# An audio tower layer on one core: identity matmuls at the start, first scores before second queries, VectorE normalising the first and last batch, GpSimd rounding the integer weights

## The reference

```python
proj = other @ W1 + readout @ W2 + b          # W1, W2: 256 x 256
h = gelu(proj)                                # 255 x 256
q, k, v = split(layernorm(h) @ qkv_w.T)       # 16 heads of 64
attn = softmax(q @ k.T * 64 ** -0.5 + bias)   # bias: emb_weight[T5 bucket(k - q)]
h = h + (attn @ v) @ o_w.T
g, u = x @ wg.T, x @ wu.T                     # x = layernorm(h); int weights / 127
h = h + (silu(g) * u) @ wd.T                  # hidden 768
```

## Time and profile before

| | us |
|---|---|
| median of 3 runs | 1811.13 (1810.99 to 1811.48) |
| the profiled execution's own time | 1811.56 |
| span of its profile | 1809.3 |
| TensorE (PE) busy | 1766.2 (98%), 17434 matmul instructions |
| VectorE (DVE) busy | 1515.6 (84%) |
| ScalarE (ACT) busy | 1396.9 (77%) |
| GpSimd (POOL) busy | 1167.8 (65%) |
| DMA from issue to landing, medians | bias rows' write 4.3, readout rows' write 2.3, bias read 4.2, pieces of w_v 3.8 |
| ScalarE's high half of a whole-number piece, 512 or 256 columns | 0.62, 0.41 |
| chain that ended last, share of the span | PE 95%, DVE 3%, ACT 1%, issue 1% |

### The profile page before, as it was taken

The page is one execution under the profiler, slowest core; times in us unless marked ns, Lnnn a source line. Parts: engine busy times, 40 slices in busy tenths (PEclk is TensorE's granted clock), DMA queues, the critical chain, the costliest instruction groups (busy, mean ns, idle before and its releaser), DMA issues.

```text
span 1809.3 us, 47269 instructions
## 1 busy us (share of the span) xinstructions
PE 1766.2 (98%) x17434; PEld 1648.3 (91%) x17434; DVE 1515.6 (84%) x4828; ACT 1396.9 (77%) x3795; POOL 1167.8 (65%) x1488
## 2 busy tenths in 40 slices
PE   7899999999999999999999999999999999999996
PEld 5789999999999999999999999999999999999995
DVE  4888888888888888888888888888889888889884
ACT  4877778777778777787777787777787777877873
POOL 2566567666667666667666667666667666667664
PEclk8999999999999999999999999999999999999998
DMA  5200000000000000000000000000000000000000
GB/s 181 71 11 16 16 10 9 14 16 16 16 7 11 16 16 16 16 4 14 16 16 16 16 4 13 16 16 16 16 5 13 16 16 16 16 5 13 8 7 13
DMA packets 26761, 34.13 MB, mean 19 GB/s; under 512 B 3457, under 2 KB 20370, under 8 KB 26530
## 3 DMA queue, kind: packets, MB, share of 16 engines
q1 hardware_dynamic: 26368, 30.95, 5.7%
q10 hardware_dynamic: 98, 0.07, 0.0%
q0 software_dynamic: 64, 0.07, 0.0%
HBM read 22.65 MB, written 8.42 MB: 17 GB/s over the span
## 4 chain that ended last, share of the span: by engine, by line
PE 95%; DVE 3%; ACT 1%; issue 1%; POOL 0%; DMA 0%; POOLq 0%; ACTq 0%; DVEq 0%
PE ps L480 57%; PE ps L561 14%; PE ps L537 13%; PE ps L550 7%; PE ps L489 3%; PE ps L505 2%; DVE prob L958 1%; DVE pT L966 1%; ACT prob L786 0%; POOL normed L410 0%; ACT pT L793 0%; DMA emb_sb<-emb 0%; DVE wu L897 0%; ACT xt L753 0%; DVE v L944 0%
## 5 line engine op out<-in xcount | busy, mean ns | idle before, releaser
L419 POOL TENSOR_TENSOR prob<-prob,inv 128x510 f32<-128x510 f32 x512 | 524.8, 1039 | 371.6 <-DVE inv L971 371.6
L793 ACT ACTIVATE pT<-ps 128x512 fp32r<-128x512 f32 x512 | 278.5, 597 | 322.4 <-PE ps L550 322.3
L786 ACT ACTIVATE prob<-prob,neg_top 128x255 f32<-128x255 f32 x1024 | 506.8, 502 | 5.0 <-DVE neg_top L958 4.7
L958 DVE CUSTOM_DVE_ANT_0 prob<-ps,bias 128x255 f32<-128x255 f32 x1024 | 380.1, 420 | 98.8 <-PE ps L537 91.5
L480 PE MATMUL ps<-xnT,wqk 128*128 128x256 f32 x3072 | 417.0, 285 | 2.9 <-DVE qk L936 1.5
L480 PEld LDWEIGHTS ps<-xnT,wqk 128*128 128x128 f32 x3072 | 381.8, 189 | 15.2 <-issue 1.8
L966 DVE TENSOR_TENSOR pT<-ps,pT 128x512 fp32r<-128x512 f32 x512 | 334.5, 685 | 1.5 <-ACT pT L793 1.5
L561 PE MATMUL ps<-pT,v 128*128 128x256 f32 x2048 | 294.9, 287 | 20.3 <-DVE pT L966 11.2
L561 PEld LDWEIGHTS ps<-pT,v 128*128 128x128 f32 x2048 | 263.7, 190 | 37.6 <-issue 31.8
L537 PE MATMUL ps<-qk 64*128 64x256 f32 x3072 | 252.5, 297 | 0.8 <-DVE neg_top L958 0.8
L537 PEld LDWEIGHTS ps<-qk 64*128 64x128 f32 x3072 | 198.9, 186 | 35.7 <-issue 1.8
(11 more groups left out here) (93 smaller groups left out, 2592.0 us busy)
## 6 DMA issues: line engine op xcount, KB each, us to landing
xt<-x_cols SPq DMA_DIRECT2D x32, 256.0 KB, 2.6
out<-xt SPq DMA_DIRECT2D x32, 128.0 KB, 1.7
r_rows<-readout_rows SPq DMA_DIRECT2D x30, 128.0 KB, 2.9
out<-xt SPq DMA_DIRECT2D x32, 112.0 KB, 1.8
bias<-bias_rows SPq DMA_DIRECT2D x8, 384.0 KB, 4.2
staged<-w_qk SPq DMA_DIRECT2D x8, 256.0 KB, 4.3
staged<-w_v SPq DMA_DIRECT2D x4, 256.0 KB, 3.8
staged<-w_o SPq DMA_DIRECT2D x4, 256.0 KB, 4.9
```

The lines of the kernel that those rows point to most:

```text
L419: pool.tensor_tensor(pr, pr, by, ALU.mult).then_inc(prob_done, 1)
L786: ex = act.activation(pr, pr, ACT.Exp, bias=neg_top[:, g % 2, hh, t:t + 1], scale=-1.0, accum_out=total[:, g % 2, hh, t:t + 1])
L793: act.activation(transposed(0, half), transposed_in(half), ACT.Copy).then_inc(pT_hi, 1)
L958: ins = dve.tensor_tensor_reduce(prob[:, g % 2, hh, t, 0:S], ps[:, bank_s[hh], t * T:t * T + S], falling(2 * g + hh, WINDOW - 1 - b0), 1.0 ...
```

## The change

- TensorE: `keep_busy(n)` issues n matmuls of the 128 x 128 identity by itself, into the bank of queries and keys, whose result nobody reads. `keep_busy(8)` runs first of all, as soon as the identity is made; `keep_busy(5)` stands after the last batch's transposes in `finish`. The bias rows come after `tokens(0)`, and the transposes of batch 0 before the readout rows of all batches. In step 0 `queries_keys(0, 1)` comes after `values(0, 0)` and `scores(0, 0)`. In steps 256 to 259 `down(30)` comes after `project`.
- VectorE: normalises batch 0 and batch 31 (the first and the last layer norm alone), in place of GpSimd. In step 0 it does the low half of `values(0, 0)` and the bias of pair 0 before the low half of pair 1. `output(30)` moves from step 258 to 259, after the statistics of batch 31. The low halves of pieces 16 to 26 come one step later.
- GpSimd: writes the high halves of pieces 16 to 26 (`integer_high`, a tensor_copy from int32 to the rounded format) at the end of steps 3 to 9, where ScalarE wrote them. Its two DMAs go to ScalarE's queue, the one of the bias rows behind gelu(0), that of the readout rows behind the loading of the table for the exponential, ahead of step 0.
- ScalarE: pieces 2, 4 and 5 earlier in the start; the table for the exponential is loaded after the high half of queries and keys of pair 0, not before; `sum_lo` one step later.
- SyncE's queue: piece 5 is asked for before the bias rows.

```diff
@@ -198,6 +198,7 @@
 POOL_PIECES = (13, 14, 15)
+FIRST_INT = min(integer_pieces)
@@ -217,6 +218,7 @@
 piece_hi = sem("piece_hi")
+int_hi = sem("int_hi")
@@ -348,9 +350,10 @@
         load_piece(QK_FIRST)
+        load_piece(QK_FIRST + 1)
...
         load_bias(0)
-        for n in range(NST, len(pieces)):
+        for n in range(V_FIRST, len(pieces)):
@@ -386,8 +389,6 @@
         pool.memset(prob[:], 0.0).then_inc(consts, 1)
-        pool.wait_ge(rel_out, 1)
-        pool.dma_start(rel_dram[:, 0:REL], rel_sb[:]).then_inc(rel_stored, 16)
@@ -431,10 +432,11 @@
+        def integer_high(n):
+            pool.wait_ge(piece_in[n % NST], 16 * (n // NST + 1))
+            pool.tensor_copy(pieces[n][1], stage(n)).then_inc(int_hi, 1)
...
         layer_rstd(0, 0)
-        normalise(0, 0)
-        pool.wait_ge(r_out, 1)
-        pool.dma_start(r_dram, r_sb[:]).then_inc(r_stored, 16)
@@ -464,9 +466,11 @@
                     piece_low(n)
+            for n in PIECES_AT.get(G, ()):
+                if n >= FIRST_INT:
+                    integer_high(n)
...
         run(step)
-        normalise(1, B - 1)
@@ -497,6 +501,10 @@
             pe.matmul(dst, ones_row[:], b_row[:], start=False, stop=True).then_inc(row_mm, 1)
...
+        def keep_busy(n):
+            for _ in range(n):
+                pe.matmul(ps[:, bank_qk, 0:P], ident[:], ident[:], start=True, stop=True)
@@ -654,6 +662,9 @@
             def transpose_banks_free():
+                if G == 1:
+                    pe.wait_ge(pre_done, 2)
+                    pe.wait_ge(r_out, 1)
@@ -680,10 +691,11 @@
-            if pair(G + 1):
+            if pair(G + 1) and G > 0:
...
                 queries_keys(*pair(G + 1))
-            early()
+            if i < B:
+                early()
@@ -693,9 +705,13 @@
                 project(bb, gg)
+            if i == B:
+                early()
...
                 scores(i, g)
+            if G == 0:
+                queries_keys(0, 1)
@@ -703,29 +719,29 @@
             norm_transposed(1, B - 1)
+            keep_busy(5)
...
+        pe.wait_ge(consts, 5)
+        keep_busy(8)
+        pe.wait_ge(r_in, 48)
+        readout_row(0)
+        pe.wait_ge(w1_in, 16)
+        tokens(0)
...
                   ).then_inc(rel_mm, 1)
-        pe.wait_ge(r_in, 48)
-        pe.wait_ge(consts, 5)
-        readout_row(0)
-        pe.wait_ge(w1_in, 16)
-        tokens(0)
...
         tokens(1)
+        norm_transposed(0, 0)
...
                   ).then_inc(r_mm, 1)
-        norm_transposed(0, 0)
         queries_keys(0, 0)
-        pe.wait_ge(pre_done, 2)
-        pe.wait_ge(r_out, 1)
@@ -833,9 +849,11 @@
                 tanh(i - 1, 5)
+            if G == 0:
+                values_hi(0, 0)
...
                 queries_keys_hi(*pair(G + 1))
-            if g == 0 and i < B:
+            if g == 0 and 0 < i < B:
@@ -845,8 +863,8 @@
                 norm_hi(0, i + 1)
-            for n in PIECES_AT.get(G - 1, ()):
-                if n in integer_pieces:
+            for n in PIECES_AT.get(G - 2, ()):
+                if n >= FIRST_INT:
@@ -859,7 +877,8 @@
             for n in PIECES_AT.get(G, ()):
-                piece_high(n)
+                if n < FIRST_INT:
+                    piece_high(n)
@@ -869,17 +888,21 @@
         piece_high(1)
+        piece_high(2)
         gelu(0)
+        act.wait_ge(rel_out, 1)
+        act.dma_start(rel_dram[:, 0:REL], rel_sb[:]).then_inc(rel_stored, 16)
+        piece_high(3)
         row_copied(1)
-        piece_high(2)
-        piece_high(3)
+        piece_high(4)
+        piece_high(5)
...
         gelu(1)
+        queries_keys_hi(0, 0)
...
         act.activation(table[:, 0:1], table[:, 1:2], ACT.Exp).then_inc(table_set, 1)
-        queries_keys_hi(0, 0)
-        piece_high(4)
-        piece_high(5)
+        act.wait_ge(r_out, 1)
+        act.dma_start(r_dram, r_sb[:]).then_inc(r_stored, 16)
@@ -892,7 +915,10 @@
             _, hi, lo, _, _, _, scale = pieces[n]
-            dve.wait_ge(piece_hi, n + 1)
+            if n < FIRST_INT:
+                dve.wait_ge(piece_hi, n + 1)
+            else:
+                dve.wait_ge(int_hi, n - FIRST_INT + 1)
@@ -923,6 +949,14 @@
             ins.then_inc(ln_var[n], 1)
...
+        def normalise(n, batch):
+            dve.wait_ge(ln_rstd[n], count(1, batch))
+            src = token_tile(batch)
+            for t in range(TT):
+                ins = dve.tensor_scalar(normed[:, t, :], src[:, t, :], mean_var[:, n, t, 0:1],
+                                        rstd[:, n, t:t + 1], ALU.subtract, ALU.mult)
+            ins.then_inc(ln_done[n], 1)
@@ -1020,7 +1054,7 @@
                 layer_sums(0, i + 1, gelu_done)
-            if g == 2 and i >= 2:
+            if g == 2 and 2 <= i < B:
@@ -1043,22 +1077,31 @@
                 gating(i - 1, 5)
+            if G == 0:
+                values_lo(0, 0)
+                add_bias(0, 0, 0)
...
                 queries_keys_lo(*pair(G + 1))
-            if g == 0 and i < B:
+            if g == 0 and 0 < i < B:
...
                 layer_var(1, i - 1)
+            if g == 3 and i == B:
+                output(B - 2)
+                normalise(1, B - 1)
...
                 heads_added(*pair(G - 2))
-            if pair(G):
+            if pair(G) and G > 0:
...
             for n in PIECES_AT.get(G, ()):
-                if n not in POOL_PIECES:
+                if n < FIRST_INT and n not in POOL_PIECES:
+                    piece_low(n)
+            for n in PIECES_AT.get(G - 1, ()):
+                if n >= FIRST_INT:
@@ -1070,23 +1113,24 @@
+        piece_low(0)
+        piece_low(1)
+        pre_gelu(0)
...
                           ).then_inc(rel_out, 1)
-        pre_gelu(0)
-        piece_low(0)
...
         layer_var(0, 0)
-        piece_low(1)
...
         piece_low(3)
+        normalise(0, 0)
         pre_gelu(1)
+        norm_lo(0, 0)
+        piece_low(4)
+        piece_low(5)
+        queries_keys_lo(0, 0)
...
         dve.tensor_copy(r_sb[:], ps[0:B, bank_t[0], 0:D]).then_inc(r_out, 1)
-        norm_lo(0, 0)
-        queries_keys_lo(0, 0)
-        piece_low(4)
-        piece_low(5)
```

## The result

The changed kernel takes 1801.09 us (median of 6, 1800.01 to 1802.67) against 1811.31 (1810.84 to 1813.84): ratio 0.9939, 95% interval 0.9928 to 0.9949, 10.2 us less (the quotient of the two medians alone would be 0.9944). Forecast were 11.7 less and 1799.4, in a range of 1796.0 to 1804.5. The profiled execution took 1802.05, its span 1799.9, so span against span it is 9.4 us. Of all executions in this document one, of e1, took 7500.4 us for a reason that no trace shows; it is left out of e1's ratio.

A forecast was written before the change was run, and what follows sets the result against it. TensorE, busy 90% or more except at the edges, bounds the kernel; chains at both ends can move the time. -8.7 - 0.5 - 2.5 = -11.7 from 1811.13 gives 1799.4 us, range 1796.0 to 1804.5.

The forecast's parts named there:

- The start: Up to the second bias of pair 0: earlier high clock, VectorE's shorter normalise and transposes before readout rows, -8.7 us.
- DMAs hidden: In the start, pieces 10 and 11 land 3.8 us after issue, before ScalarE needs them, with 0.4 us to spare.
- Steps 2 to 12: After the start: ScalarE's relief gains little, VectorE's low halves only move; net -0.5 us, between -1.5 and +1.
- rival C: GpSimd's copies of integer weights collide with VectorE's low halves, +4.9 us on VectorE's chain, 1804.3 us; chance 0.18.
- The end: Last 30 us: residual earlier, gate_up all at the full clock; -2.5 us, or -4.2 if down is fast too.
- transposes 0: At the end, the last transposes start no earlier, since down runs partly at 1.2 GHz, +1.7; with the full clock -1.7.
- keep_busy(5): In finish, its ten records, 1.2 us fast, are hidden in the 1.35 us of the two halves; slow would cost 1.0.
- A: Rival: at the end down stays fast, its idle times costing nothing; -13.4 us, 1797.7 us; chance 0.20.
- B: Rival: at the start the clock does not rise earlier; 1809.3 us, no change; chance 0.08.
- D: Rival: GpSimd's copies become the bound in steps 5 to 7, each 4.0 us; 1815 us; chance 0.02.

The follow-up runs named there:

- e1: The changed kernel without the eight identity matmuls at the start: ratio 0.9957 against the kernel before, +3.3 us on the changed kernel.
- e5: The changed kernel with both normalises (batches 0 and 31) back on GpSimd: ratio 0.9960, +3.8 us on the changed kernel.
- e3: The kernel before with the eight identity matmuls ahead of everything, nothing else: ratio 0.9994.
- e11: The changed kernel with SyncE's queue waiting for the readout rows behind piece 11 in place of piece 9: ratio 0.9928, -2.0 us on the changed kernel.
- e7: The changed kernel with integer weights rounded by ScalarE again, low halves and sums in their old steps: ratio 0.9938, -0.2 us on the changed kernel.
- e12: The changed kernel with e10 and e11 together, plus 8 identity matmuls in the idle time of step 2: 1796.31 us, ratio 0.9909.
- e6: The changed kernel with step 0 in its old order (queries of pair 1, values, scores) on TensorE, ScalarE and VectorE: ratio 0.9939.
- e9: The changed kernel with identity matmuls (8, 7 and 8) in the idle times of steps 256, 257 and 258: ratio 0.9921, -3.3 us on the changed kernel.
- e10: The changed kernel with identity matmuls (8, 7, 10) in the drain's idle times, down(30) ahead of the last project and output(30) in step 258: ratio 0.9919.
- e2: The changed kernel without the five identity matmuls in finish: ratio 0.9945, +1.1 us on the changed kernel.

## Why the prediction was right, and where it was off

**The start, -8.7: right, by its steps.** tokens(0) ended at 9.96 (9.7 said), the transposes started at 15.27 (15.15), queries_keys at 17.38 (17.45) and fast, the second bias at 26.13 (26.3). VectorE's normalise is 0.73 us for two, nearly the 0.76 of the two-input operation. The Trainium skill ("VectorE: DVE Perf Modes", section Mode 2x_2P) would have had about 0.4, by the prediction's estimate; the trace does not agree, and the nearest row was the better price. e1 and e5 show that both parts count: without the identity matmuls +3.3, with GpSimd's normalise +3.8, each just clear of its 3 us, while in the old kernel the identity matmuls alone are not told from nothing (e3). What the prediction did not say is that normalise mattered through the clock (5.3 us at the second bias in e5) more than through its own 1.7. The rest of the start (transposes ahead of the readout rows, the later table load, the DMAs on ScalarE's queue, the order of the pieces) was never run alone. That the second bias hit 26.3 within 0.2 is in part luck: the same code gave 25.0 to 26.1 in eight traces, since the clock rose at different moments behind the identity matmuls. The first clock record of a trace is that rise: it stands at 7.6 us in the changed kernel and at 4.8 to 7.6 in the eight traces, at 11.3 without the identity matmuls (e1), and at 13.6 before.

**DMAs hidden, 0.4 us to spare: wrong.** The prediction took 3.8 us for a piece to land (and its 29.3 for piece 11 should have been 25 + 3.8 = 28.8, by its own numbers). In the changed kernel w_v's median is 5.8, behind the readout rows and the bias; ScalarE waited 1.32 us, and e11 gives 0.7 us at the first values_probs; its 2.0 in the time is not told from nothing. "A late one costs what it is late" was the right rule and the landing the wrong term.

**Steps 2 to 12, -0.5: was +1.2 in the two traces, and is not told from 0.** The spread of the same code in other traces is as large (76.8 to 78.4 before, 77.5 to 79.0 after). The moved low halves and the casts are not it (e7), nor a collision: for rival C the low halves would have had to grow by 4.9 us on VectorE's chain, and they are 8.8 against 8.6. The late piece is real and small. A low clock stands from 93 to 100 us after, where the old trace had one from 102 to 106 behind an idle time of the same length:

```profile
102.82 2.04 PE L561 MATMUL ps<-pT,v 128*128 128x256 f32 x8 [3.07 <-DVE v L944]
```

```profile
93.88 2.05 PE L569 MATMUL ps<-pT,v 128*128 128x256 f32 x8 [3.08 <-DVE v L978]
```

But the old trace had two more low stretches, at 44 and 65 us, and the new one only one more, at 35 us: in sum the low clock lasts 10.2 us in both, so it is no ready explanation of a difference. e12, which filled step 2 and took the late piece away, has 75.8 us here, less than any trace without that.

**The end, -2.5: was -1.5 in the two traces, and -1.5 to -3.9 over all of them.** As foretold down(30) ran slow, normalise gave nothing there, and gate_up was fast throughout; from the transposes to the end it was 18.2 us before and is 15.4. The term that was off is "transposes 0": from the last scores to the transposes it was 21.0 us before and 22.2 in the changed kernel's trace. The prediction priced a low clock for down alone (1.7 us; down took 4.52 in place of 3.05) and took steps 256 and 257 over unchanged from a trace with a low clock from 1774.8 to 1778.2 only; here the clock fell in step 256 and made both values and both projects slow too. That is a matter of chance as well: with the same code the values of step 256 took 2.05 us in the changed kernel and 1.19 in e6 and e7, and down(30) 3.82 to 4.52. So the low clock in the drain as a cost is shown (e9, e10, e12), and where in the drain it falls is not foreseeable from these traces. A sum from one trace on each side can't be nearer than that, and that the time came within 1.7 us of the forecast is partly luck.

**keep_busy(5)** was called hidden and is (1.28 us within the wait for the halves); that it is needed was not said. e2's trace shows that gate_up is half slow without it, though its time does not.

**The rivals.** A was the wrong way round (the low clock cost more, not less), B did not come, C is refuted, D was far off: a cast of 128x512 takes 0.60 us, below the 0.8 taken from twice the cast of 128x256. The Trainium skill ("SBUF — State Buffer", section SBUF: two separate sides) speaks of a lock between GpSimd and VectorE's operations with two inputs in SBUF. Single low halves of 0.95 us, where a like one took 0.42, stand in the trace, but e7 without the casts has such ones too, and the sums are 8.8 and 8.6 us: no cost of a lock by the casts is shown. The lower end of the range, 1796.0, is 0.6 us under what its own terms give (1797.7 - 0.8 - 0.3).

## What to carry to other kernels

Where a chain of small tiles surrounds a matmul engine at the start and end of a program, price each idle time of TensorE twice: by its length, and by the slow matmuls behind it. Which of the two, a shorter gap or filler matmuls, is enough depends on the code around: in the changed start the clock held without the fillers (e1) and fell with them behind GpSimd's normalise (e5). Filling the waits of the drain gave 3.3 us for one matmul loop, a third of the whole change. And take several traces where the clock is at stake: the same code differed by 1.0 to 1.6 us in each stretch above, as much as the terms in dispute. Relief of an engine that no chain goes through (6.4 us of ScalarE) is worth nothing, and a transfer that moves in a queue must be priced with what is loaded beside it, not by its median elsewhere.

## What the runs showed of the hardware that was not expected

The length of an idle time alone did not decide the clock. Two of 1.4 and 1.5 us with 0.66 us of transposes between were followed by 1.2 GHz (e2), while in the old trace single ones of 2.1 and 2.74 us were not. The same 3.1 us in step 10 were followed by a low clock from 102.3 to 105.7 us before and from 92.9 to 99.8 after, and the same 2.51 us in step 256 by a slow `values_probs` in the changed kernel (2.05 us) and a fast one in e6 and e7 (1.19).

The Trainium skill ("TensorE: Matmul & The Clock Gate", section What's actually happening) says that throttled is the resting state and activity releases it; the slow first tokens(0) and the fast one after 3.78 us of identity matmuls agree. A stretch ahead of a trace's first clock record is shown as 1.00 with nothing recorded in it, so there only the lengths of the matmuls tell. Matmuls of an identity, nearly all zeros, were enough: with them tokens(0) took 1.99 us, without them 3.78 (e1), and the drain filled with them stayed at 1.00 (e9). The eight identity matmuls in the old kernel (e3) went with twelve runs spread over 8.8 us, where the kernel before spread 23 over 4.5; why is not shown.
